# A graph layer on one core: edges and zeros are loaded into the buffers first, and the gathers add onto them

## The chip, the cores and the metric

The kernel runs on one core of a Trainium2 chip. Its time is the device time of one execution in microseconds; before the change the median of three runs is 2434.07 us (2429.45 to 2435.82). The engines of a core work side by side and meet at semaphores: TensorE (PE in the profile, PEld its weight loads), VectorE (DVE), ScalarE (ACT), GpSimd (POOL) and SyncE (SP), which here only issues transfers. Sixteen DMA engines carry the transfers of all of them.

## The reference

A graph with N = 12500 nodes of D = 64 features and E = 212500 edges, sorted by destination, goes through one attention layer:

```
h_trans = x @ Watt.T + Watt_b
e   = sum(h_trans[dst] * tanh(h_trans[src] + edge_attr), axis=-1) / 8
e   = leaky_relu(e, 0.2)
p   = exp(e - segment_max(e, dst)[dst])
alpha   = p / (segment_sum(p, dst)[dst] + 1e-9)
h_neigh = segment_sum(x[src] * alpha, dst)
h   = leaky_relu((x + h_neigh) @ W1.T + W1_b + (x * h_neigh) @ W2.T + W2_b)
out = layernorm(x + h)
```

The term that the change touches is `h_trans[src] + edge_attr`: a gathered row of 64 numbers plus the edge's own row of 64.

## The kernel before, in words

Since the edges are sorted by destination, the kernel walks over blocks of 128 destination nodes, 98 of them. A block takes a window of 19 tiles of 128 edges (MAIN = 17 and TAIL = 2); a tail tile that the block does not need is not gathered. Tiles are worked on in five chunks of four (the last has three), and in three pieces of two chunks each for the coarser steps.

Set-up: x is loaded and copied into hx, TensorE and VectorE compute h_trans, and SP writes a table in HBM whose row n is h_trans of node n (64 numbers) and x of node n (64 numbers), 512 bytes together. A search finds each block's first edge.

The main part is a software pipeline over blocks (`pipeline`, L330). Every engine runs its own `step` or `gather` for each block, four blocks to a turn of a loop, and an engine's order is just the order of its code. In one step it works for several blocks: `b`, the block before it `prev`, the one before that `before`, then `third`, and for `nxt` and `ahead` (b + 1 and b + 2).

- SP (`step`, L455) waits until block b - 2 is scored (`scored`) and its ids are set (`ids_set`). Then it loads the edges of b into one of two buffers `edge` (`load_edges`), the row of destinations of b (`load_row`), and the indices of block b + 2 (`load_indices`).
- GpSimd (`gather`, L543) has four buffers `got`. For each of the 19 tiles it issues one indirect DMA (L560): 128 table rows by the source indices into `got[:, g, 0:128]`. Before chunks 0, 2 and 4 it waits until block n - 4 has been weighted (`weighted`), since that frees the buffer.
- VectorE adds the gathered h_trans onto the edges, chunk by chunk (`add`, L1084), ScalarE takes tanh (`tanh`, L662), and VectorE multiplies by the expanded h_trans[dst] from PSUM and sums (`dot`, L1095). For prev it computes maxima by scans, ScalarE takes the exponential, and VectorE weights the x half of the gathered rows (`weight_rows`, L1143), splits them into three bf16 parts, and TensorE sums them by a one-hot matrix.
- The second half of the gathered row, `got[:, :, 64:128]`, is x[src]; its last column, 128, holds ones.

After the last block the rows are normalised and stored.

Of the kernel before, what the change touches and what calls it, by code (L numbers as in the profile page):

```python
# [22 lines left out]
ALU = mybir.AluOpType  # L23
ACT = mybir.ActivationFunctionType
# [5 lines left out]
P = 128  # L30
MAIN = 17
# [3 lines left out]
BUFS = 4  # L35
# [15 lines left out]
def at_block(turn, k):  # L51

    return Block(turn * BUFS + k, k % BUFS, k % 2, turn + k // BUFS, turn * 2 + k // 2, isinstance(turn, int))


def gnn_layer(nc, x, src, dst, edge_attr, w1, b1, w2, b2, watt, batt, out):
# [31 lines left out]
    with ExitStack() as ctx:  # L88
        def sb(name, shape, dt=F32):
            return ctx.enter_context(nc.sbuf_tensor(name, shape, dt))  # L90
# [4 lines left out]
        def sem(name):  # L95
            return ctx.enter_context(nc.semaphore(name))
# [60 lines left out]

        src_i = [sb(f"src_i{k}", [P, TILES], I32) for k in range(BUFS)]
        dst_i = [sb(f"dst_i{k}", [P, TILES], I32) for k in range(BUFS)]
        edge = [sb(f"edge{k}", [P, TILES, D]) for k in range(2)]  # L160
        got = [sb(f"got{k}", [P, TILES, 2 * D + 1]) for k in range(BUFS)]

# [108 lines left out]
        h3_ready = sem("h3_ready")  # L271

        index_in = [sem(f"index_in{k}") for k in range(BUFS)]
        edge_in = [sem(f"edge_in{k}") for k in range(2)]
        gathered = [[sem(f"gathered{k}_{c}") for c in range(NC)] for k in range(BUFS)]
        row_in = [sem(f"row_in{k}") for k in range(2)]
        hot_built = by_chunk("hot_built")
# [115 lines left out]
        def _(sp):  # L393
# [33 lines left out]
            def first_edge(b):  # L427
                return sp.value_load(start_i[0:1, b.n:b.n + 1] if b.known else start_i[0:1, bass.ds(b.n, 1)],
                                     min_val=0, max_val=E - WINDOW)
# [6 lines left out]
                                 vector[bass.ds(o + MAIN * P, TAIL * P)].rearrange("(g p) -> p g", p=P),  # L436
                                 allow_slow_non_contiguous=True).then_inc(index_in[b.four], 16)

            def load_edges(b, o):
                sp.dma_start(edge[b.two][:, 0:MAIN, :],  # L440
                             edge_attr[bass.ds(o, MAIN * P), :].rearrange("(p g) d -> p g d", g=MAIN))\
                    .then_inc(edge_in[b.two], 16)
                sp.dma_start(edge[b.two][:, MAIN:TILES, :],
                             edge_attr[bass.ds(o + MAIN * P, TAIL * P), :].rearrange("(g p) d -> p g d", p=P))\
                    .then_inc(edge_in[b.two], 16)

            def load_row(b, o):
                ends = dst[bass.ds(o, MAIN * P)].rearrange("(a p g) -> a p g", a=1, g=MAIN)[:, :, 0:MAIN:MAIN - 1]
                sp.dma_start(row_i[b.two][:, 0:2 * P].rearrange("a (p e) -> a p e", e=2), ends,
                             allow_slow_non_contiguous=True).then_inc(row_in[b.two], 16)  # L450
                sp.dma_start(row_i[b.two][:, 2 * P:ROW],
                             dst[bass.ds(o + MAIN * P, TAIL * P)].rearrange("(a n) -> a n", a=1))\
                    .then_inc(row_in[b.two], 16)

            def step(third, before, prev, b, nxt, ahead):  # L455
                if not exists(b):
                    return
                edges_at = first_edge(b)
                indices_at = first_edge(ahead) if exists(ahead) else None
                if follows(b, 2):  # L460

                    sp.wait_ge(scored[NC - 1], b.n - 1)
                    sp.wait_ge(ids_set, b.n - 1)
                load_edges(b, edges_at)
                load_row(b, edges_at)
                if exists(ahead):
                    load_indices(ahead, indices_at)

            def general_tile(t):

# [7 lines left out]
            with sp.If(is_general(sp)):  # L478
# [3 lines left out]
                for k in range(PIECES):  # L482
                    a, z = k * PIECE, (k + 1) * PIECE if k < PIECES - 1 else BLOCKS
                    sp.dma_start(state_piece[k][:, 0:z - a, :],
                                 state[a * P:z * P, :].rearrange("(b p) d -> p b d", p=P)).then_inc(g_back, 16)
            with sp.Else():
                for n in range(2):
                    load_indices(at_block(0, n), first_edge(at_block(0, n)))
                pipeline(sp, step)

            def store(a, z):
# [14 lines left out]
        def _(pool):  # L506
# [9 lines left out]

            for k in range(BUFS):
                pool.memset(got[k][:, MAIN:TILES, 0:2 * D], 0.0).then_inc(consts, 1)

            def place_x(k):  # L520

# [21 lines left out]
            def gather(third, before, prev, b, nxt, ahead):  # L543
                if not exists(b):
                    return
                if follows(b, BUFS):

                    pool.wait_ge(weighted[0], b.n - (BUFS - 1))
                pool.wait_ge(index_in[b.four], (b.fours + 1) * 64)
                n = pool.value_load(count_i[0:1, b.n:b.n + 1] if b.known else count_i[0:1, bass.ds(b.n, 1)],  # L550
                                    min_val=0, max_val=E)
                for c, tiles in enumerate(CHUNKS):
                    if c in (2, 4) and follows(b, BUFS):


                        pool.wait_ge(consts, 11)
                        pool.wait_ge(weighted[c // 2], b.n - (BUFS - 1))  # L557
                    for g in tiles:
                        def rows():
                            pool.indirect_dma_start(got[b.four][:, g, 0:2 * D], None, table,  # L560
                                                    bass.IndirectOffsetOnAxis(ap=src_i[b.four][:, g:g + 1], axis=0))\
                                .then_inc(gathered[b.four][c], 16)
                        if g < MAIN:
                            rows()
                        else:

                            with pool.If(n > g * P):  # L567
                                rows()
                            with pool.Else():
                                pool.inc_swdge_sem([gathered[b.four][c]], [16], mode="add")  # L570
# [42 lines left out]
        def _(act):  # L613
# [44 lines left out]

            def tanh(b, c):
                a, z = cols(c)  # L660
                act.wait_ge(added[c], b.n + 1)
                act.activation(edge[b.two][:, a:z, :], edge[b.two][:, a:z, :], ACT.Tanh).then_inc(tanh_done[c], 1)  # L662

            def set_ids(b):

# [269 lines left out]
        def _(dve):  # L935
# [140 lines left out]
                    dst_rel[:, a:z, :].rearrange("p g (z a) -> p g z a", z=1).to_broadcast([P, z - a, P // 2, 2]),  # L1076
                    ALU.is_equal).then_inc(hot_built[c], 1)

            def add(b, c):
                a, z = cols(c)  # L1080
                if c == 0:
                    dve.wait_ge(edge_in[b.two], (b.twos + 1) * 32)
                dve.wait_ge(gathered[b.four][c], (b.fours + 1) * (16 * (z - a)))
                dve.tensor_tensor(edge[b.two][:, a:z, :], edge[b.two][:, a:z, :], got[b.four][:, a:z, 0:D],  # L1084
                                  ALU.add).then_inc(added[c], 1)

            def dot(b, c):

                a, z = cols(c)
# [112 lines left out]
            def step(third, before, prev, b, nxt, ahead):  # L1202
                if exists(third):
                    residual(third, 0)
                if exists(prev):
                    finish_scores(prev)
                if exists(third):
                    residual(third, 1)
                if exists(b):
                    add(b, 0)  # L1210
                if exists(nxt):
                    place(nxt)
                    build_hot(nxt, 0)
                    build_hot(nxt, 1)
                if exists(prev):
                    scan_row(prev)
                if exists(b):
                    add(b, 1)
                    dot(b, 0)
                if exists(nxt):  # L1220
                    build_hot(nxt, 2)
                    build_hot(nxt, 3)
                    build_hot(nxt, 4)
                if exists(prev):
                    exponents(prev)
                if exists(b):
                    add(b, 2)
                    dot(b, 1)
                if exists(prev):
                    for p in range(NP):  # L1230
                        weight_rows(prev, p)
                if exists(b):
                    add(b, 3)
                if exists(prev):
                    for p in range(NP):
                        rest(prev, 0, p)
                if exists(b):
                    dot(b, 2)
                    add(b, 4)
# [108 lines left out]
```

## Time and profile before

| | |
|---|---|
| median of three runs | 2434.07 us |
| the profiled execution | 2435.8 us |
| its span | 2434.1 us |
| GpSimd busy | 1824.6 us, 75% |
| VectorE busy | 1799.4 us, 74% |
| TensorE busy | 1051.8 us, 43% |
| ScalarE busy | 875.6 us, 36% |
| gathers (L560) | 1716, 1045 ns each |
| additions (L1084) | 490, 407 ns each |

The profile gives for each engine how long it was busy, then the chain of waits: from the last instruction back, at each step to what released it. That chain tells which engine's work sets the end. For a group of instructions the profile gives the number, the busy time, the mean of one, and the idle time of the engine just before them with what ended it. "issue" means that nothing in the profile explains the idle time: the engine was being handed its next instruction, for example.

### The profile page before, as it was taken

The page shows a single profiled execution, that of the slowest core. Times are in us where ns is not written, and L with a number is a line of the kernel's source. Part 1 is how long each engine was busy: PE and PEld are TensorE (multiplying, and loading weights), DVE is VectorE, ACT ScalarE, POOL GpSimd, SP SyncE. Part 2 cuts the span into 40 slices and gives each one's busy share as a digit, 9 for nine tenths or more (in the row PEclk, how much of TensorE's full clock was granted, in tenths as well). Part 3 has the DMA queues.
Part 4 walks back from the last instruction along what each step waited for, and adds up shares of the span by engine and source line. Part 5 has one row for each costly group of instructions (what it writes and reads, how often), then busy time and mean ns, then how long its engine had stood idle before and what let it go on. Part 6 is the DMA issues. An engine that isn't in the chain of part 4 may idle for free.

```text
span 2434.1 us, 41241 instructions
## 1 busy us (share of the span) xinstructions
PE 1051.8 (43%) x10542; PEld 905.3 (37%) x10542; DVE 1799.4 (74%) x8215; ACT 875.6 (36%) x2120; POOL 1824.6 (75%) x1741
## 2 busy tenths in 40 slices
PE   3334444444434444454444454444344444444441
PEld 3334333334433333343333343343343333433331
DVE  5577778678777778687687787787777776877866
ACT  4343333334243333333344243343333333343431
POOL 2777777777777777777777777777777777777773
PEclk8565556655565565556565566566555655666555
DMA  7323323232322323233232332323323232323322
GB/s 193 88 74 78 80 71 81 69 82 70 81 78 71 82 70 82 70 82 80 72 81 70 82 80 70 81 69 81 81 70 81 69 81 70 79 72 79 81 60 55
DMA packets 243239, 191.45 MB, mean 79 GB/s; under 512 B 190278, under 2 KB 202876, under 8 KB 243100
## 3 DMA queue, kind: packets, MB, share of 16 engines
q0 software_dynamic: 55072, 113.24, 17.4%
q1 hardware_dynamic: 188028, 76.98, 13.6%
q14 instruction: 129, 1.06, 0.2%
q8 instruction: 10, 0.16, 0.0%
HBM read 180.47 MB, written 9.60 MB: 78 GB/s over the span
## 4 chain that ended last, share of the span: by engine, by line
POOL 68%; issue 22%; POOLq 7%; SPq 1%; DMA 1%; DVE 1%; PE 0%; ACT 0%; DVEq 0%; ACTq 0%
POOL got L560 67%; POOLq L570 4%; POOLq L550 2%; SPq L422 1%; DMA triple<-in_dst 1%; POOL hx L374 0%; POOLq L567 0%; PE ps_acc L869 0%; POOLq L88 0%; POOL hx L376 0%; POOL hx L524 0%; POOLq L557 0%; DMA got<-table,src_i 0%; POOLq L337 0%; DMA dst_i<-in_dst 0%
## 5 line engine op out<-in xcount | busy, mean ns | idle before, releaser
L560 POOL DMA_INDIRECT got<-table,src_i x1716 | 1794.0, 1045 | 550.3 <-issue 550.3
L662 ACT ACTIVATE edge<-edge 128x256 f32<-128x256 f32 (+1 forms) x490 | 198.2, 404 | 1072.8 <-DVE edge L1084 1063.7
L1084 DVE TENSOR_TENSOR edge<-edge,got 128x256 f32<-128x256 f32 (+1 forms) x490 | 199.3, 407 | 297.2 <-DMA got<-table,src_i 293.8
L876 PE MATMUL ps_misc<-ident,sum_prod 128*128 128x128 f32 x98 | 46.5, 474 | 727.5 <-DVE sum_prod L1172 727.5
L657 ACT ACTIVATE hotT<-ps_hot 128x1024 bf16<-128x1024 bf16 (+1 forms) x294 | 236.6, 841 | 343.6 <-PE ps_hot L817 343.6
L831 PEld LDWEIGHTS ps_hd<-h,hotT 128*128 128x128 bf16 x5586 | 340.4, 134 | 19.5 <-issue 4.9
L831 PE MATMUL ps_hd<-h,hotT 128*128 (+1 forms) x5586 | 338.1, 242 | 4.5 <-DVE raw L1095 4.5
L1095 DVE CUSTOM_DVE_ANT_0 edge<-edge,ps_hd 128x64 f32<-128x64 f32 x1862 | 298.7, 211 | 1.4 <-PE ps_hd L831 0.4
L876 PEld LDWEIGHTS ps_misc<-ident,sum_prod 128*128 128x128 f32 x98 | 17.9, 182 | 747.0 <-DVE sum_prod L1172 747.0
L869 PE MATMUL ps_acc<-triple,hot 128*128 128x195 bf16 x1862 | 295.3, 347 | 0.3 <-DVE z L1178 0.3
L694 ACT ACTIVATE triple<-rows 128x520 bf16<-128x520 f32 (+1 forms) x588 | 284.5, 550 | 14.9 <-DVE rows L1152 11.8
L869 PEld LDWEIGHTS ps_acc<-triple,hot 128*128 128x128 bf16 x1862 | 244.2, 138 | 18.2 <-DVE z L1178 0.5
L817 PE MATMUL ps_hot<-ident,hot 128*128 128x128 bf16 x1862 | 195.1, 275 | 75.8 <-ACT hotT L657 50.9
L1143 DVE TENSOR_TENSOR rows<-got,weight 128x520 f32<-128x520 f32 (+1 forms) x294 | 155.2, 582 | 91.1 <-ACT weight L682 90.7
L817 PEld LDWEIGHTS ps_hot<-ident,hot 128*128 128x128 bf16 x1862 | 170.6, 130 | 96.5 <-issue 69.2
L1073 DVE TENSOR_TENSOR hot<-iota_h,dst_rel 128x512 bf16<-128x512 bf16 (+1 forms) x490 | 174.2, 401 | 3.4
L843 PE MATMUL ps_row<-ident,part_max 128*1 128x128 f32 x196 | 57.4, 396 | 244.1 <-DVE part_max L1109 143.3
L1152 DVE TENSOR_TENSOR rows<-rows,triple 128x520 f32<-128x520 f32 (+1 forms) x294 | 154.6, 579 | 7.7 <-ACT triple L694 7.4
L1155 DVE TENSOR_TENSOR triple<-rows,triple 128x520 bf16<-128x520 f32 (+1 forms) x294 | 154.8, 581 | 0.0
L1095 DVE DVE_READ_ACCUMULATOR2_ANT raw<- 128x1 f32 x1862 | 145.3, 78 | 0.2 <-issue 0.2
L857 PE MATMUL ps_misc<-ident,row_max 1*128 1x1 f32 x196 | 36.1, 251 | 239.5 <-issue 234.8
L857 PEld LDWEIGHTS ps_misc<-ident,row_max 1*128 1x128 f32 x196 | 30.6, 203 | 252.7 <-issue 252.7
(122 smaller groups left out, 1418.6 us busy)
## 6 DMA issues: line engine op xcount, KB each, us to landing
edge<-in_edge_attr SPq DMA_DIRECT2D x98, 544.0 KB
got<-table,src_i POOLq DMA_INDIRECT x1716, 2.5
edge<-in_edge_attr SPq DMA_DIRECT2D x98, 64.0 KB
table<-hx SPq DMA_DIRECT2D x12, 512.0 KB
row_i<-in_dst SPq DMA_DIRECT2D x196, 1.0 KB
got<-in_x SPq DMA_DIRECT2D x3, 768.0 KB, 14.4
src_i<-in_src SPq DMA_DIRECT2D x98, 8.5 KB
src_i<-in_src SPq DMA_DIRECT2D x98, 1.0 KB
```

What stands on the lines that cost most here:

```text
L560: pool.indirect_dma_start(got[b.four][:, g, 0:2 * D], None, table, bass.IndirectOffsetOnAxis(ap=src_i[b.four][:, g:g + 1], axis=0))\
L657: act.activation(hotT[b.two][:, a:z, :], ps, ACT.Copy).then_inc(hot_sb[p], 1)
L662: act.activation(edge[b.two][:, a:z, :], edge[b.two][:, a:z, :], ACT.Tanh).then_inc(tanh_done[c], 1)
L694: act.activation(parts[:, a:z, k, :], rows[:, a:z, :], ACT.Copy).then_inc(part_set[k][p], 1)
L817: last = pe.transpose(ps_hot[(b.two + p) % 2][:, k * P:(k + 1) * P], hot[b.four][:, g, :], ident16[:, :])
L831: last = pe.matmul(expanded(g), hotT[b.two][:, g, :], rhs, start=(part == 0), stop=(part == 2))
L869: last = pe.matmul(a_sum, hot[b.four][:, g, :], triple[:, g, 0:SUMS], start=(g == 0), stop=(g == TILES - 1))
L1073: dve.tensor_tensor(hot[b.four][:, a:z, :].rearrange("p g (n a) -> p g n a", a=2), iota_h[:, :].rearrange("p (z n a) -> p z n a", z=1, a=2 ...
L1084: dve.tensor_tensor(edge[b.two][:, a:z, :], edge[b.two][:, a:z, :], got[b.four][:, a:z, 0:D], ALU.add).then_inc(added[c], 1)
L1095: last = dve.tensor_tensor_reduce(out=edge[b.two][:, g, :], in0=edge[b.two][:, g, :], in1=expanded(g), scale=1.0, scalar=0.0, op0=ALU.mult ...
L1143: dve.tensor_tensor(rows[:, a:z, :], got[b.four][:, a:z, D:2 * D + 1], weight[:, a:z].rearrange("p (g d) -> p g d", d=1).to_broadcast([P, ...
L1155: dve.tensor_tensor(parts[:, a:z, 2, :], rows[:, a:z, :], parts[:, a:z, 1, :], ALU.subtract)\
```

## The change

Edges are no longer loaded into buffers of their own. SP loads them straight into the first 64 columns of the `got` buffer of the block two ahead, and a third transfer copies a row of zeros into its columns 64 to 127 (`lay_edges`, which takes the place of `load_edges`). The gathers now have `compute_op=ALU.add`: they add the table's row onto what lies there. So `got[:, g, 0:64]` becomes h_trans[src] + edge_attr, and `got[:, g, 64:128]` becomes 0 + x[src]. VectorE's `add` is gone; ScalarE's tanh waits for the gathers and reads `got`, writing `edge`, which has to be free (block b - 2 scored). GpSimd waits for the three transfers (`laid`) in place of the freed buffer, and SP now waits for the freed buffer, that is for all pieces of `weighted` of block b - 2, before it loads for block b + 2.

```
-            def load_edges(b, o):
-                sp.dma_start(edge[b.two][:, 0:MAIN, :],
+            def lay_edges(b, o):
+
+                sp.dma_start(got[b.four][:, 0:MAIN, 0:D],
                              edge_attr[bass.ds(o, MAIN * P), :].rearrange("(p g) d -> p g d", g=MAIN))\
-                    .then_inc(edge_in[b.two], 16)
-                sp.dma_start(edge[b.two][:, MAIN:TILES, :],
+                    .then_inc(laid[b.four], 16)
+                sp.dma_start(got[b.four][:, MAIN:TILES, 0:D],
                              edge_attr[bass.ds(o + MAIN * P, TAIL * P), :].rearrange("(g p) d -> p g d", p=P))\
-                    .then_inc(edge_in[b.two], 16)
+                    .then_inc(laid[b.four], 16)
+                sp.dma_start(got[b.four][:, :, D:2 * D],
+                             zeros[:, :].rearrange("p (g d) -> p g d", g=1).to_broadcast([P, TILES, D]))\
+                    .then_inc(laid[b.four], 16)
...
-                    sp.wait_ge(scored[NC - 1], b.n - 1)
+                    sp.wait_ge(zeros_set, 1)
+                    for p in range(NP):
+                        sp.wait_ge(weighted[p], b.n - 1)
                     sp.wait_ge(ids_set, b.n - 1)
-                load_edges(b, edges_at)
-                load_row(b, edges_at)
+                row_at = first_edge(b)
+                ahead_at = first_edge(ahead) if exists(ahead) else None
+                load_row(b, row_at)
                 if exists(ahead):
-                    load_indices(ahead, indices_at)
+                    load_indices(ahead, ahead_at)
+                    lay_edges(ahead, ahead_at)
...
+                sp.wait_ge(x_set, PIECES)
+                sp.wait_ge(zeros_set, 1)
                 for n in range(2):
                     load_indices(at_block(0, n), first_edge(at_block(0, n)))
+                    lay_edges(at_block(0, n), first_edge(at_block(0, n)))
...
-                if follows(b, BUFS):
-
-                    pool.wait_ge(weighted[0], b.n - (BUFS - 1))
+                pool.wait_ge(laid[b.four], (b.fours + 1) * 48)
...
                             pool.indirect_dma_start(got[b.four][:, g, 0:2 * D], None, table,
-                                                    bass.IndirectOffsetOnAxis(ap=src_i[b.four][:, g:g + 1], axis=0))\
-                                .then_inc(gathered[b.four][c], 16)
+                                                    bass.IndirectOffsetOnAxis(ap=src_i[b.four][:, g:g + 1], axis=0),
+                                                    compute_op=ALU.add).then_inc(gathered[b.four][c], 16)
...
-                act.wait_ge(added[c], b.n + 1)
-                act.activation(edge[b.two][:, a:z, :], edge[b.two][:, a:z, :], ACT.Tanh).then_inc(tanh_done[c], 1)
+                act.wait_ge(gathered[b.four][c], (b.fours + 1) * (16 * (z - a)))
+                if follows(b, 2):
+
+                    act.wait_ge(scored[c], b.n - 1)
+                act.activation(edge[b.two][:, a:z, :], got[b.four][:, a:z, 0:D], ACT.Tanh).then_inc(tanh_done[c], 1)
```

On SP, this stood in one step of the pipeline before: the wait, the edges of b, its row, and the first indices of b + 2.

```order
L440 ISA [waits ids_set,scored_4]
L440 DMA edge<-in_edge_attr 128x1088
L443 ISA
L443 DMA edge<-in_edge_attr 128x2x64
L449 REGISTER_ALU
L449 DMA row_i<-in_dst 1x256x1
L451 REGISTER_ALU
L451 DMA row_i<-in_dst 1x256
L433 REGISTER_ALU
L433 DMA src_i<-in_src 128x17
L435 ISA
L435 DMA src_i<-in_src 128x2x1
```

Now the step begins with the wait and the row (the line numbers have moved):

```order
L430 TENSOR_LOAD start_i [waits weighted_2,weighted_1,ids_set,weighted_0,zeros_set]
L430 ISA x2
L430 TENSOR_LOAD start_i
L430 ISA x2
L455 REGISTER_ALU
L455 DMA row_i<-in_dst 1x256x1
```

and it ends with the indices of b + 2 and the three loads of b + 2:

```order
L435 DMA src_i<-in_src 128x17
L437 ISA
L437 DMA src_i<-in_src 128x2x1
L435 DMA dst_i<-in_dst 128x17
L437 DMA dst_i<-in_dst 128x2x1
L443 ISA
L443 DMA got<-in_edge_attr 128x17x64
L446 ISA
L446 DMA got<-in_edge_attr 128x2x64
L449 DMA got<-zeros 128x19x64
```

The wait has moved from the scores of b - 2 to its weighting, and the edges from the front of the step to its end, for a block two later; their form has changed from rows of 1088 numbers to 17 runs of 64.

On VectorE, an early step before: the scores of prev, the first addition of b, the one-hots of nxt, the scans, the second addition, the first score of b (`L1095`).

```order
L1103 SCALAR_TENSOR_TENSOR score<-raw 128x19
L1106 SCALAR_TENSOR_TENSOR run_max<-gap,score 128x17
L1109 SCALAR_TENSOR_TENSOR part_max<-gap,run_max 128x17
L1084 TENSOR_TENSOR edge<-edge,got 128x256
L1062 TENSOR_SCALAR dst_rel<-dst_i,base 128x38
L1065 TENSOR_SCALAR base<-base 128x1
L1073 TENSOR_TENSOR hot<-iota_h,dst_rel 128x512 x2
L1115 SCALAR_TENSOR_TENSOR row_max<-row_gap,ps_row 1x512
L1117 SCALAR_TENSOR_TENSOR row_max<-row_gap,row_max 1x512
L1084 TENSOR_TENSOR edge<-edge,got 128x256
L1095 ISA edge,raw<-edge,ps_hd 128x64
```

The same place now:

```order
L1103 SCALAR_TENSOR_TENSOR score<-raw 128x19
L1106 SCALAR_TENSOR_TENSOR run_max<-gap,score 128x17
L1109 SCALAR_TENSOR_TENSOR part_max<-gap,run_max 128x17
L1070 TENSOR_SCALAR dst_rel<-dst_i,base 128x38
L1073 TENSOR_SCALAR base<-base 128x1
L1081 TENSOR_TENSOR hot<-iota_h,dst_rel 128x512 x2
L1115 SCALAR_TENSOR_TENSOR row_max<-row_gap,ps_row 1x512
L1117 SCALAR_TENSOR_TENSOR row_max<-row_gap,row_max 1x512
L1095 ISA edge,raw<-edge,ps_hd 128x64
```

Only the additions are gone; nothing else on VectorE changes its place. On GpSimd the order of the gathers is the same, with the other waits.

## Rows read from the trace of the kernel before

**Rows 1.** The page, busy time: us, share of the span, instructions.

```profile
PE 1051.8 (43%) x10542; PEld 905.3 (37%) x10542; DVE 1799.4 (74%) x8215; ACT 875.6 (36%) x2120; POOL 1824.6 (75%) x1741
```

**Rows 2.** The page, the chain that ended last, by engine and by line.

```profile
POOL 68%; issue 22%; POOLq 7%; SPq 1%; DMA 1%; DVE 1%; PE 0%; ACT 0%; DVEq 0%; ACTq 0%
POOL got L560 67%; POOLq L570 4%; POOLq L550 2%; SPq L422 1%; DMA triple<-in_dst 1%; POOL hx L374 0%; POOLq L567 0%; PE ps_acc L869 0%; POOLq L88 0%; POOL hx L376 0%; POOL hx L524 0%; POOLq L557 0%; DMA got<-table,src_i 0%; POOLq L337 0%; DMA dst_i<-in_dst 0%
```

**Rows 3.** Groups of GpSimd: count | busy us, mean ns | idle before.

```profile
L560 POOL DMA_INDIRECT got<-table,src_i x1716 | 1794.0, 1045 | 550.3 <-issue 550.3
...
L529 POOL DMA_INDIRECT triple<-in_dst,row_idx x1 | 1.3, 1287 | 16.2 <-issue 16.2
```

**Rows 4.** Line 560: ns min/median/max, first and last start; who waited; landing.

```profile
L560 POOL DMA_INDIRECT got<-table,src_i x1716: 940/944/2311, 57.4 to 2372.8; - x191
...
  DVE edge L1084: 293.8, 152
...
DMA to landing us min/median/max: 2.4/2.5/4.5
```

**Rows 5.** GpSimd in order of time: start us, us, instruction, idle before.

```profile
57.45 1.48 POOL L560 DMA_INDIRECT got<-table,src_i  x1 [27.70 <-issue]
...
1207.80 0.94 POOL L560 DMA_INDIRECT got<-table,src_i  x1 [0.30 <-issue]
1209.05 1.15 POOL L560 DMA_INDIRECT got<-table,src_i  x1 [0.30 <-issue]
1210.50 0.94 POOL L560 DMA_INDIRECT got<-table,src_i  x1 [0.30 <-issue]
```

**Rows 6.** The page, VectorE's additions.

```profile
L1084 DVE TENSOR_TENSOR edge<-edge,got 128x256 f32<-128x256 f32 (+1 forms) x490 | 199.3, 407 | 297.2 <-DMA got<-table,src_i 293.8
```

**Rows 7.** Count loads up to 1200 us, then from 1200; scores up to 1207.

```profile
L550 POOLq TENSOR_LOAD <-count_i x49: 283/290/302, 56.1 to 1180.1; - x49
...
L550 POOLq TENSOR_LOAD <-count_i x5: 285/288/296, 1203.1 to 1296.7; - x5
...
L1103 DVE SCALAR_TENSOR_TENSOR score<-raw x48: 166/169/181, 84.8 to 1206.0; 128x19 f32<-128x19 f32 x48
```

**Rows 8.** VectorE in order of time, parts of one step.

```profile
1208.14 0.43 DVE L1084 TENSOR_TENSOR edge<-edge,got 128x256 f32<-128x256 f32 x1
...
1208.95 0.76 DVE L1073 TENSOR_TENSOR hot<-iota_h,dst_rel 128x512 bf16<-128x512 bf16 x2
1209.63 1.20 DVE L1115 TENSOR_TENSOR_SCAN row_max<-row_gap,ps_row 1x512 f32<-1x512 f32 x1
...
1217.09 1.58 DVE L1143 TENSOR_TENSOR rows<-got,weight 128x520 f32<-128x520 f32 x3 [1.58 <-ACT weight L682]
```

**Rows 9.** SP's transfers of one step, the first and the last of eight.

```profile
1200.66 0.34 SPq L440 DMA_DIRECT2D edge<-in_edge_attr  x1
...
1204.63 0.38 SPq L435 DMA_DIRECT2D dst_i<-in_dst  x1
```

**Rows 10.** Stretches of 256-byte pieces: ..., PEclk, DMA share, GB/s last.

```profile
10.00:15.00 5.00, 0.00 (x0) 0.00 (x0) 0.00 (x0) 0.00 (x0) 0.00 (x0) 1.00 0.97 167
...
2416.00:2420.00 4.00, 0.00 (x0) 0.00 (x0) 3.09 (x1) 0.00 (x0) 3.92 (x2) 0.50 0.96 218
```

**Rows 11.** Stretches about one load of edges, the same columns.

```profile
1200.00:1202.00 2.00, 0.83 (x16) 0.67 (x13) 1.16 (x9) 0.00 (x0) 1.39 (x2) 0.50 0.32 70
1202.00:1204.00 2.00, 0.00 (x0) 0.00 (x0) 0.00 (x0) 0.00 (x0) 1.44 (x2) 0.50 0.92 319
1204.00:1206.00 2.00, 0.00 (x0) 0.00 (x0) 0.11 (x1) 0.00 (x0) 1.64 (x2) 0.50 0.65 99
...
1208.00:1224.00 16.00, 7.04 (x75) 6.07 (x72) 13.70 (x64) 8.34 (x21) 12.50 (x12) 0.71 0.20 49
```

**Rows 12.** The main part as one stretch, the same columns.

```profile
80.00:2370.00 2290.00, 1010.73 (x10214) 869.48 (x10214) 1718.95 (x8012) 828.67 (x2029) 1773.14 (x1697) 0.59 0.30 76
```

**Rows 13.** The page, DMA queues: GpSimd's is q0, SP's is q1.

```profile
q0 software_dynamic: 55072, 113.24, 17.4%
q1 hardware_dynamic: 188028, 76.98, 13.6%
```

**Rows 14.** SP in the set-up: three loads of x, block 0's first index load.

```profile
5.90 15.14 SPq L396 DMA_DIRECT2D got<-in_x  x3
...
52.04 0.37 SPq L433 DMA_DIRECT2D src_i<-in_src  x1
```

More of the change, by code:

```diff
@@ L159, in gnn_layer @@
         dst_i = [sb(f"dst_i{k}", [P, TILES], I32) for k in range(BUFS)]
+        zeros = sb("zeros", [P, D])
         edge = [sb(f"edge{k}", [P, TILES, D]) for k in range(2)]
@@ L273, in gnn_layer @@
         index_in = [sem(f"index_in{k}") for k in range(BUFS)]
-        edge_in = [sem(f"edge_in{k}") for k in range(2)]
+        zeros_set = sem("zeros_set")
+        laid = [sem(f"laid{k}") for k in range(BUFS)]
         gathered = [[sem(f"gathered{k}_{c}") for c in range(NC)] for k in range(BUFS)]
@@ L457, in step @@
                     return
-                edges_at = first_edge(b)
-                indices_at = first_edge(ahead) if exists(ahead) else None
                 if follows(b, 2):
-                    sp.wait_ge(scored[NC - 1], b.n - 1)
+                    sp.wait_ge(zeros_set, 1)
+                    for p in range(NP):
+                        sp.wait_ge(weighted[p], b.n - 1)
                     sp.wait_ge(ids_set, b.n - 1)
-                load_edges(b, edges_at)
-                load_row(b, edges_at)
+                row_at = first_edge(b)
+                ahead_at = first_edge(ahead) if exists(ahead) else None
+                load_row(b, row_at)
                 if exists(ahead):
-                    load_indices(ahead, indices_at)
+                    load_indices(ahead, ahead_at)
+                    lay_edges(ahead, ahead_at)
             def general_tile(t):
@@ L518, in _ @@
                 pool.memset(got[k][:, MAIN:TILES, 0:2 * D], 0.0).then_inc(consts, 1)
+            pool.memset(zeros[:, :], 0.0).then_inc(zeros_set, 1)
             def place_x(k):
@@ L552, in gather @@
                 for c, tiles in enumerate(CHUNKS):
-                    if c in (2, 4) and follows(b, BUFS):
-                        pool.wait_ge(consts, 11)
-                        pool.wait_ge(weighted[c // 2], b.n - (BUFS - 1))
                     for g in tiles:
@@ L1077, in build_hot @@
                     ALU.is_equal).then_inc(hot_built[c], 1)
[L1079 to L1085, printed above, removed]
             def dot(b, c):
@@ L1208, in step @@
                     residual(third, 1)
-                if exists(b):
-                    add(b, 0)
                 if exists(nxt):
@@ L1217, in step @@
                 if exists(b):
-                    add(b, 1)
                     dot(b, 0)
@@ L1226, in step @@
                 if exists(b):
-                    add(b, 2)
                     dot(b, 1)
@@ L1231, in step @@
                         weight_rows(prev, p)
-                if exists(b):
-                    add(b, 3)
                 if exists(prev):
@@ L1238, in step @@
                     dot(b, 2)
-                    add(b, 4)
                 if exists(before):
```

## The prediction

> **What bounds the kernel now.** I read the busy shares and the chain of waits first, then the largest group of the engine that the chain names, then its single instructions, and last the transfers. GpSimd and VectorE are busy for almost the same share, 75% and 74% [rows 1], so the shares do not decide. The chain does: 67% of it is the gather at L560, and 22% is "issue" [rows 2]. There are 1716 gathers, 1045 ns each on average, with 550.3 us of idle time before them [rows 3]. Less the 27.7 us before the first one [rows 5] that is 522.6/1715 = 305 ns a gap. The first gather starts at 57.4 us and the last at 2372.8 [rows 4], and 1716 x 1.045 + 522.6 = 2316 us fills that whole stretch: GpSimd never waits for a buffer there. It issues gathers back to back, 0.94 us and 0.30 us of gap [rows 5]. Around it lie 57 us of set-up and some 60 us of last block and normalisation. VectorE waits for gathers 152 times, 293.8 us together [rows 4]; it is the follower. So the price of this change is what it does to one gather on GpSimd, times 1716, and what it puts ahead of the first gather.
>
> **VectorE's additions.** 490 go, 199.3 us [rows 6]. VectorE follows, so this is worth nothing in the stretch; in the last block it takes off about a microsecond. ScalarE's tanh then waits for the gather itself, one hop less, also beside the gathers. I count 0.
>
> **What GpSimd waits for.** Three waits for free buffers per block become one wait for three loads. Every gap that I see in the stretch is 0.30 us with or without such a wait before it [rows 5], so 0 for their removal. The new wait must be met in time. SP now issues the loads of block n+4 after all three pieces of block n are weighted. Blocks from 0: GpSimd reads the count of block 48 at 1180.1 us, of 49 at 1203.1 and of 53 at 1296.7 [rows 7], so of block 51 at about 1250. VectorE finishes the scores of block 47 at 1206.0 (the 48th) [rows 7] and its weighting at 1217.09 + 1.58 = 1218.7 [rows 8]. SP then issues the row and index loads, which take it about 4 us (the first of its transfers at 1200.66, the last at 1204.63) [rows 9], and then the three loads. With 10 us for these they have landed by 1233, 17 us before they are wanted. A longer gather only widens that. Behind SP's wait are queued the row of block b, wanted by ScalarE at the end of its step, and the indices two blocks ahead; they go some 15 us later than now and still have a block to spare. 0.
>
> **The added transfers.** Edges went as 4352-byte rows (128 x 1088); now they go as 17 pieces of 256 bytes to a partition, with 2 x 64 beside them, and zeros add 19 more. That is (19 + 19) x 128 = 4864 pieces a block, 304 on each of 16 DMA engines. Two places show 256-byte pieces alone. While x is loaded the engines are 97% busy at 167 GB/s: 16 x 0.97 x 256 / 167 = 23.8 ns a piece. While the output is stored they are 96% busy at 218 GB/s: 18.0 ns [rows 10]. So a block's loads hold each DMA engine for 5.5 to 7.2 us. What they replace is the burst at 1200 to 1206: (0.32 + 0.92 + 0.65) x 2 us less the 0.20 of the stretch behind it, 2.6 us [rows 11]. The share over the stretch is 0.30 [rows 12], or 7.1 us of a block of 23.6 us (2316/98). The new load would be 7.1 - 2.6 + 5.5 to 7.2 = 10 to 11.7 us, and if the adding gathers hold the engines twice as long, another 17.4% of the span [rows 13] = 4.1 us: 16 of 23.6. Hidden. SP is free too: 3072 such pieces hold it about 5.05 us (15.14/3) when its queue is full [rows 14], so 4864 take at most 8 us of SP's 23.6.
> Ahead of the first gather nothing hides them. SP starts block 0's index loads at 52.04 us and the first gather starts at 57.45, behind them [rows 5, 14]. Behind those four loads come now the three of block 0: 5.5 to 7.2 us of transfer, and perhaps 2 us more for issue and landing (a gather needs 2.5 to land [rows 4]), part of it beside the indices' own landing. I take 7 us, within 4 to 10.
>
> **The adding gather.** No row shows one. From below: the DMA engines do the addition and GpSimd writes as many instructions for them as now, +0 ns; below nothing is possible only through what runs beside (see the rivals). From above: it has to name twice as many transfers, since the destination is read too, and all of its 944 ns is such naming: +944 ns, 1716 x 0.944 = 1620 us. The nearest row is the other indirect DMA of this kernel, L529: 99 rows of 6800 bytes, 1287 ns [rows 3] where 128 rows of 512 bytes take 944 [rows 4]. It is a gather whose transfers are put together differently from those at L560, and the only one. I take it as the size of what a different form costs: +343 ns, 1716 x 0.343 = 589 us. It is a guess between ends far apart and the largest uncertainty here; +343 sits in the lower half of 0 to 944, which suits a cost of which part must be fixed.
>
> **Sum.** The profiled execution took 2435.8 us in all, 1.7 us above its span and the median of the runs. 2435.8 - 0 + 7 + 589 = 3032, less 1.7: **3030 us**. A block would take 23.6 + 17.5 x 0.343 = 29.6 us, still GpSimd's own time.
>
> **Rivals.**
> *The gather costs what it did.* Then only the 7 us remain: 2434 + 7 = 2441 us. For it: the same 128 rows, the same indices, and an addition done elsewhere. Against it: something has to name the read of the destination. It falls on both sides of 0.3% (7.3 us), which is about what a measurement of this kernel can tell from no change.
> *The gather's naming doubles.* 2434 + 7 + 1620 = 4061 us. For it: with no wait in the stretch, the 944 ns look like work that goes by rows (940 at least, 944 in the median [rows 4]). Against it: a part must be fixed for an instruction.
> The Trainium skill, page "Collectives: The Full Stack", section on the fold count, says that an adding transfer needs two source reads, and that two read descriptors are issued for each chunk where a copy has one. By that rule the time tends to this rival; no row here shows an adding transfer.
> *Faster.* One mechanism: the gathers are longer than their floor because VectorE works beside them. The mean is 1045 ns and the floor 944, 101 x 1716 = 173 us. If VectorE's traffic does that and the additions carry their part of it, 199.3 of 1799.4 us, then 19 us go; less 7, 2422 us. If they carried all of it, 2434 + 7 - 173 = 2268 us. It decides from 7 us on, 4 ns a gather. Against it: the gather at 1207.80 takes 0.94 us with the addition at 1208.14 inside it, and the one at 1209.05 takes 1.15 us with no addition in it but one-hots and a scan [rows 5, 8].
> The Trainium skill, page "SBUF — State Buffer", section "Who interferes with whom", has a two-input addition take only the shared read path, while building descriptors needs the write path. By that rule the trace agrees, and nothing would come back.
> *The DMA engines become the bound.* The adding gathers would have to hold them for more than 23.6 - (11.7 - 4.1) = 16 us a block, where the plain ones hold 4.1: four times as long. At five times, 20.5 + 7.6 = 28 us a block, 98 x 4.5 = 440 us more: 2880 us. For it: each 512-byte row would be fetched, added and written in turn. Against it: 0.30 share now [rows 12].
>
> **How the numbers follow.** Forecast (a gather longer by 50 to 700 ns, own range 2525 to 3640) 0.42; doubled 0.15; unchanged 0.26, half of it within 0.3% and half slower; faster 0.10; the DMA engines as bound 0.07. Slower by over 0.3%: 0.42 + 0.15 + 0.13 + 0.07 = 0.77; within 0.13; faster 0.10. The range goes from 2425, which keeps the unchanged case and a little of the faster one, to 4060, the doubled case; outside are the larger gains and a gather that more than doubles.
>
> **What the changed profile would show.** Right: the gather's floor about 1.29 us at the same 0.30 gap, the chain on it for over two thirds, VectorE's busy time down by 199 us and its waits for gathers up, the first gather about 7 us later, the DMA share at about 0.5 to 0.6 of a shorter block. Wrong: a floor of 0.94 (unchanged), of 1.9 (doubled), a mean nearer the floor (faster), or a DMA share near 1 with gathers that land late and GpSimd held at its wait for the loads.

## The result and the profile after

The changed kernel takes 3353.38 us (median of four runs, 3351.42 to 3357.83), the kernel before 2434.95 us beside it: ratio 1.379, 95% interval 1.3771 to 1.3808. The profiled execution took 3357.83 us, its span 3356.1.

The page of the changed kernel, the busy time and the chain of waits, which answer to [rows 1, 2]:

```profile
PE 1008.5 (30%) x10542; PEld 874.0 (26%) x10542; DVE 1652.1 (49%) x7725; ACT 851.6 (25%) x2120; POOL 2741.4 (82%) x1742
...
POOL 76%; issue 17%; POOLq 4%; PE 1%; DMA 1%; SPq 0%; DVE 0%; ACT 0%; DVEq 0%; ACTq 0%
```

GpSimd carries more of the chain than before (76% for 68%), and VectorE has fallen from 74% to 49% of the span. The gathers (L565 now), in the view of groups and then of the line, which answer to [rows 3, 4] (ns min/median/max, then the first and last start):

```profile
L565 POOL DMA_INDIRECT got<-table,src_i x1716 | 2710.6, 1580 | 558.1 <-issue 558.1
```
```profile
L565 POOL DMA_INDIRECT got<-table,src_i x1716: 1531/1540/2510, 65.3 to 3296.8; - x191
...
  ACT edge L670: 2373.4, 435
...
DMA to landing us min/median/max: 3.1/3.3/6.3
```

The same 1716 gathers take 1580 ns each in place of 1045, and the median 1540 in place of 944. The gaps are the same: 558.1 us less the 35.5 before the first is 522.6 us, as before. Where the 922 us of span went is a sum of three terms, from the first and last start of a gather here and in [rows 4]: the first gather starts 65.3 - 57.4 = 7.9 us later; from the first to the last start it is 3231.5 us in place of 2315.4, 916 us more (1716 x 0.535 = 918); and behind the last start it is 59.3 us in place of 61.3, 2 us less.

GpSimd in order of time, at the start and in the middle (answers to [rows 5]):

```profile
65.32 1.60 POOL L565 DMA_INDIRECT got<-table,src_i  x1 [35.50 <-issue]
...
1501.85 1.54 POOL L565 DMA_INDIRECT got<-table,src_i  x1 [0.30 <-issue]
1503.69 1.54 POOL L565 DMA_INDIRECT got<-table,src_i  x1 [0.30 <-issue]
1505.54 1.96 POOL L565 DMA_INDIRECT got<-table,src_i  x1 [0.30 <-issue]
```

The DMA queues, then the main part as one stretch (the last two columns are DMA share and GB/s), which answer to [rows 13, 12]:

```profile
q0 software_dynamic: 247264, 113.24, 28.0%
q1 hardware_dynamic: 628636, 138.00, 22.3%
```
```profile
80.00:3280.00 3200.00, 970.33 (x10241) 840.57 (x10241) 1571.38 (x7524) 806.15 (x2030) 2682.24 (x1699) 0.58 0.50 73
```

GpSimd's queue moves the same 113.24 MB in 247264 packets in place of 55072: 1716 x 144 against 1716 x 32, with 160 others in both, so 112 packets more for each gather of 128 rows. They hold the engines 0.280 x 3356 = 940 us in place of 0.174 x 2434 = 424 us, 2.2 times as long. Still the share of all transfers over the main part is 0.50, so the engines have half their time free. SP's loads of one block, and how long edges and zeros take to land in the median:

```profile
1511.67 0.60 SPq L443 DMA_DIRECT2D got<-in_edge_attr  x1
1512.45 1.81 SPq L446 DMA_DIRECT2D got<-in_edge_attr  x1
1514.31 0.65 SPq L449 DMA_DIRECT2D got<-zeros  x1
```
```profile
got<-zeros SPq DMA_DIRECT2D x98, 608.0 KB, 6.0
got<-in_edge_attr SPq DMA_DIRECT2D x98, 544.0 KB, 4.9
```

### The profile page after: what moved, and what is told of

Read it like the earlier page. It is cut to its first block, busy times and chain, and to the rows that moved or that the text cites. A ratio compares the mean times of both kernels' runs of the same rounds, so it can differ in the third digit from the quotient of the medians.

```text
span 3356.1 us, 41105 instructions
## 1 busy us (share of the span) xinstructions
PE 1008.5 (30%) x10542; PEld 874.0 (26%) x10542; DVE 1652.1 (49%) x7725; ACT 851.6 (25%) x2120; POOL 2741.4 (82%) x1742
## 3 DMA queue, kind: packets, MB, share of 16 engines
q0 software_dynamic: 247264, 113.24, 28.0%
## 4 chain that ended last, share of the span: by engine, by line
POOL 76%; issue 17%; POOLq 4%; PE 1%; DMA 1%; SPq 0%; DVE 0%; ACT 0%; DVEq 0%; ACTq 0%
POOL got L565 75%; POOLq L575 2%; POOLq L560 1%; DMA triple<-in_dst 0%; POOL hx L376 0%; POOLq L572 0%; PE ps_row L789 0%; PE ps_acc L877 0%; PE ps_hd L789 0%; SPq L424 0%; PE ps_hd L778 0%; DMA got<-zeros 0%; POOLq L88 0%; POOL hx L378 0%; DMA got<-table,src_i 0%
## 5 line engine op out<-in xcount | busy, mean ns | idle before, releaser
L565 POOL DMA_INDIRECT got<-table,src_i x1716 | 2710.6, 1580 | 558.1 <-issue 558.1
L670 ACT ACTIVATE edge<-got 128x256 f32<-128x256 f32 (+1 forms) x490 | 199.3, 407 | 2373.9 <-DMA got<-table,src_i 2373.4
L1095 DVE CUSTOM_DVE_ANT_0 edge<-edge,ps_hd 128x64 f32<-128x64 f32 x1862 | 299.0, 213 | 749.5 <-issue 741.8
L839 PEld LDWEIGHTS ps_hd<-h,hotT 128*128 128x128 bf16 x5586 | 328.8, 132 | 14.4
L839 PE MATMUL ps_hd<-h,hotT 128*128 (+1 forms) x5586 | 324.8, 238 | 0.0
L877 PE MATMUL ps_acc<-triple,hot 128*128 128x195 bf16 x1862 | 282.6, 337 | 0.3 <-DVE z L1178 0.3
L889 PE MATMUL ps_acc<-w12T,sum_prodT 128*128 128x64 f32 x196 | 67.3, 447 | 634.6 <-ACT sum_prodT L706 634.6
L877 PEld LDWEIGHTS ps_acc<-triple,hot 128*128 128x128 bf16 x1862 | 234.2, 133 | 16.8 <-DVE z L1178 0.5
L889 PEld LDWEIGHTS ps_acc<-w12T,sum_prodT 128*128 128x128 f32 x196 | 49.0, 311 | 663.3 <-ACT sum_prodT L706 663.3
L1143 DVE TENSOR_TENSOR rows<-got,weight 128x520 f32<-128x520 f32 (+1 forms) x294 | 155.3, 583 | 68.4 <-ACT weight L690 68.4
L1095 DVE DVE_READ_ACCUMULATOR2_ANT raw<- 128x1 f32 x1862 | 149.3, 80 | 1.3 <-issue 0.7
L1117 DVE TENSOR_TENSOR_SCAN row_max<-row_gap,row_max 1x512 f32<-1x512 f32 x98 | 118.7, 1211 | 3.4
L1115 DVE TENSOR_TENSOR_SCAN row_max<-row_gap,ps_row 1x512 f32<-1x512 f32 x98 | 117.7, 1201 | 0.3 <-PE ps_row L853 0.2
```

The costliest lines, as they stand in the source:

```text
L670: act.activation(edge[b.two][:, a:z, :], got[b.four][:, a:z, 0:D], ACT.Tanh).then_inc(tanh_done[c], 1)
L839: last = pe.matmul(expanded(g), hotT[b.two][:, g, :], rhs, start=(part == 0), stop=(part == 2))
L877: last = pe.matmul(a_sum, hot[b.four][:, g, :], triple[:, g, 0:SUMS], start=(g == 0), stop=(g == TILES - 1))
L1095: last = dve.tensor_tensor_reduce(out=edge[b.two][:, g, :], in0=edge[b.two][:, g, :], in1=expanded(g), scale=1.0, scalar=0.0, op0=ALU.mult ...
L1143: dve.tensor_tensor(rows[:, a:z, :], got[b.four][:, a:z, D:2 * D + 1], weight[:, a:z].rearrange("p (g d) -> p g d", d=1).to_broadcast([P, ...
```

## The experiments

Each comparison has its own runs of the kernel before. They fell into two kinds: in one of them that kernel took 2435.08 us, as above, and in three, each on another chip, 3582.33, 3604.71 and 3615.52 us. So every result below names the kernel before beside it. A time from one kind is set against a time from the other only where GpSimd's gathers fill the run. The median durations of single gathers are read from the traces, and there both kinds agree (944 or 945 ns plain, 1540 or 1541 adding).

**Only the addition undone.** The changed kernel with plain gathers, run twice (e1_laid_plain, e8_laid_plain_again). It leaves the edges out of the scores.

```
-    bass.IndirectOffsetOnAxis(ap=src_i[b.four][:, g:g + 1], axis=0),
-    compute_op=ALU.add).then_inc(gathered[b.four][c], 16)
+    bass.IndirectOffsetOnAxis(ap=src_i[b.four][:, g:g + 1], axis=0)).then_inc(gathered[b.four][c], 16)
```

> The changed kernel with only the addition taken out of the gathers: the three loads per block, SP's wait, GpSimd's wait and the missing VectorE additions all stay. It leaves out the edges in the scores, since the plain gather overwrites them. Theory (the whole cost is the form of the gather on GpSimd): a gather takes its 0.94 us again, mean at most 1.05 us, the first gather stays at 65.3 us, time 2435 + 8 = 2443 us. Rival (the added loads or the new waits cost something in the loop): gathers with a mean above 1.1 us or gaps above 0.30 us, time above 2480 us. Second rival (VectorE's additions had lengthened the gathers): mean near 1.00 us, time near 2370 us.

Measured the first time: 3546.41 us beside 3582.33, ratio 0.9909 (0.986 to 0.9957). The waits view of this run (us in total, times, the longest):

```profile
ACT hotT L662 <- PE ps_hot L825: 2123.2, 88, 49.5
POOL got L565 <- issue: 1699.1, 1712, 40.2
```

ScalarE waited 2123 us for TensorE, and GpSimd had 1700 us of gaps, with gathers of 945 ns in the median: something else was the bound, so the run says nothing on the sum. The same kernel was run again.

> The same kernel as the first experiment (the changed kernel with plain gathers; it leaves the edges out of the scores), because the kernel before itself took 3582 us on the chip of that comparison in place of 2434, with TensorE idle for 'issue' between single matmuls. Theory (the form of the gather is the whole cost, and that chip had a limit of its own beside GpSimd): where the kernel before takes about 2434 us, this takes 2443 us, a gather 0.94 us at the least and 1.0 us on average (998 ns were seen), gaps 0.30 us. With a mean of 998 in place of 1045 ns it could be 1716 x 0.047 = 81 us less, 2362 us, if the additions had lengthened the gathers. Rival (the loads and the new wait cost something): above 2480 us.

Measured: 2419.71 us beside 2435.08, ratio 0.9938 (0.9916 to 0.9959). The gathers:

```profile
L565 POOL DMA_INDIRECT got<-table,src_i x1716: 940/945/1822, 65.0 to 2359.5; - x191
```
```profile
L565 POOL DMA_INDIRECT got<-table,src_i x1716 | 1772.7, 1033 | 557.9 <-issue 557.6 <-DMA got<-zeros 0.3
```

The whole loss is gone, with all loads, both new waits and the missing additions in place. The new wait for the loads cost GpSimd 0.3 us in 98 blocks. The expected time was 2443 us, so 23 us less than that, and 15 us less than the kernel before: gathers of 1033 in place of 1045 ns, 1716 x 0.012 = 21 us, less the 7.6 us by which the first gather starts later (65.0 us for 57.4). What shortened them this run does not tell, since the additions are gone and the loads have moved as well.

**Only the addition put in.** The kernel before with `compute_op=ALU.add` in its gathers, and the four buffers cleared once ahead; it adds onto what the buffer held.

```
+            for k in range(BUFS):
+                pool.memset(got[k][:, :, 0:2 * D], 0.0).then_inc(cleared, 1)
+            pool.wait_ge(cleared, BUFS)
...
-                                                    bass.IndirectOffsetOnAxis(ap=src_i[b.four][:, g:g + 1], axis=0))\
+                                                    bass.IndirectOffsetOnAxis(ap=src_i[b.four][:, g:g + 1], axis=0), compute_op=ALU.add)\
```

> The kernel before with only the addition put into the gathers (and the four buffers cleared once ahead, some 10 us on GpSimd). It adds onto what the buffer held, so rows pile up; edges still go to their own buffers and VectorE still adds. Theory (the form of the gather is the whole cost): floor of 1.54 us, mean 1.58 to 1.64 us, time 2435 + 10 + 1716 x (0.535 to 0.60) = 3363 to 3475 us. Rival (half of the loss comes from the loads, waits or the 256-byte pieces): mean near 1.3 us, time near 2900 us.

Measured: 3358.97 us (two runs) beside 3582.33, ratio 0.9375 (0.9357 to 0.9393): the kernel before was of the slower kind there. The comparison that counts is with the changed kernel, 3353.38 us, from which it differs by 0.2%; that kernel keeps its time from chip to chip (last experiment). It lies just under the 3363 us that I had expected at the least. The gathers:

```profile
L564 POOL DMA_INDIRECT got<-table,src_i x1716 | 2707.1, 1578 | 524.9 <-issue 517.9 <-DVE rows L1147 7.0
```

With the two together, the form of the gather is the cost, and it alone makes the loss. VectorE's additions are still there and the mean is 1578 ns, where it is 1580 without them and with the new loads: beside adding gathers these two changes together give nothing.

**What the cost of an adding gather goes by.** The same two kernels (buffers cleared ahead) with gathers of 64 and of 16 rows, the other rows left out, and one with adding gathers of 128 rows of 256 bytes, which fetch x in place of the table. This is the edit for 64 adding rows:

```
-                            pool.indirect_dma_start(got[b.four][:, g, 0:2 * D], None, table,
-                                                    bass.IndirectOffsetOnAxis(ap=src_i[b.four][:, g:g + 1], axis=0))\
+                            pool.indirect_dma_start(got[b.four][0:64, g, 0:2 * D], None, table,
+                                                    bass.IndirectOffsetOnAxis(ap=src_i[b.four][0:64, g:g + 1], axis=0), compute_op=ALU.add)\
```

> The kernel before with each gather fetching 64 rows in place of 128 (the other half of each tile is left out), buffers cleared once ahead. It shows which part of the 944 ns goes by rows. If all of it goes by rows: a floor of 472 ns; if it is fixed for the instruction: 944 ns. I expect about 650 ns, which would be 350 ns fixed and 4.6 ns a row; GpSimd would then still be the bound or nearly, with a time of 1900 to 2100 us where VectorE's own 20 us a block allow it.

> The same with the adding gather: 64 rows, buffers cleared once ahead, rows pile up. If the added 596 ns of the floor (1.54 against 0.944 us) go by rows (a second read is named for every row), the difference to the plain gather of 64 rows is 298 ns, floor about 0.95 us. If they are fixed for an adding instruction, the difference is 596 ns, floor about 1.25 us.

> The kernel before with adding gathers that fetch rows of 64 numbers (256 bytes) from x in place of 128 from the table, 128 rows each; buffers cleared once ahead. It leaves out the h half. If the cost goes by instruction and row, the floor stays at 1.54 us and the time at 3359 us; if it goes by bytes (the transfer holds GpSimd up), the floor falls towards 1.25 us.

> The kernel before with gathers of 16 rows (the other 112 of each tile left out), buffers cleared once ahead. The plain gather took 944 ns for 128 rows and 908 for 64. A straight line gives 872 ns + 0.56 a row: 881 ns here. If the line is not straight (work in groups of rows), something else, down to 600 ns.

> The same with adding gathers of 16 rows. They took 1540 ns for 128 rows and 1412 for 64; a straight line gives 1284 ns + 2.0 a row: 1316 ns here, that is 412 ns fixed and 1.4 ns a row more than the plain one. If what the addition costs goes by rows after all, near 900 ns.

The line of the gathers in these five, in this order (ns min/median/max):

```profile
L564 POOL DMA_INDIRECT got<-table,src_i x1716: 902/908/1506, 63.3 to 3472.5; - x191
```
```profile
L564 POOL DMA_INDIRECT got<-table,src_i x1716: 1403/1412/2385, 64.2 to 3128.1; - x191
```
```profile
L564 POOL DMA_INDIRECT got<-in_x,src_i x1716: 1531/1540/2720, 64.2 to 3310.8; - x191
```
```profile
L564 POOL DMA_INDIRECT got<-table,src_i x1716: 842/848/2211, 64.3 to 2225.1; - x191
```
```profile
L564 POOL DMA_INDIRECT got<-table,src_i x1716: 1307/1317/2386, 64.5 to 2946.6; - x191
```

| rows in a gather | plain, ns | adding, ns | difference |
|---|---|---|---|
| 16 | 848 | 1317 | 469 |
| 64 | 908 | 1412 | 504 |
| 128 | 944 | 1540 | 596 |

The adding form costs 469 ns more already at 16 rows and only 127 beyond that at 128: four fifths of what the addition costs are there at 16 rows and look fixed for the instruction. For 64 rows I had set 298 ns (by rows) against 596 (fixed); 504 lies between, nearer to fixed. The straight line gave 1316 for 16 adding rows (1317 measured) but 881 for 16 plain ones (848). My 650 ns for 64 plain rows was far off. Bytes do not matter to the adding gather: half-width rows take the same 1540 ns. Nor is it the number of packets. At 16 rows GpSimd's queue has 55072 of them in both forms (plain first), and the adding gather still takes 469 ns longer:

```profile
q0 software_dynamic: 55072, 14.84, 2.7%
```
```profile
q0 software_dynamic: 55072, 14.84, 5.1%
```

The times were 3587.23, 3191.02, 3373.57, 2287.56 and 3009.51 us; the first two stood beside 3582.33 us for the kernel before, the others beside 2435.08. Each of the five is a single run. Even 16 plain rows bring the kernel only to 2288 us: with a gather of 955 ns on the mean (848 in the median) and a gap of some 300, GpSimd is still the bound.

**A dose.** The changed kernel with the addition in even tiles only (odd tiles lose their edges).

```
-                                                    compute_op=ALU.add).then_inc(gathered[b.four][c], 16)
+                                                    compute_op=ALU.add if g % 2 == 0 else ALU.bypass).then_inc(gathered[b.four][c], 16)
```

> The changed kernel with the addition only in the gathers of even tiles, some 890 of the 1716 (odd tiles lose their edges). If each adding gather costs its own 1580 - 1033 = 547 ns on GpSimd and nothing else, 2420 + 890 x 0.547 = 2907 us. If a change between the two forms costs something, or the DMA side of an adding gather holds up the next one, more than that: over 2950 us.

Measured: 2929.79 us (one run) beside 3604.71. Line, queue, and three gathers in order of time:

```profile
L565 POOL DMA_INDIRECT got<-table,src_i x1716: 978/1532/2388, 65.5 to 2868.9; - x191
```
```profile
q0 software_dynamic: 153968, 113.24, 23.7%
```
```profile
1501.88 1.54 POOL L565 DMA_INDIRECT got<-table,src_i  x1 [0.30 <-issue]
1503.73 0.98 POOL L565 DMA_INDIRECT got<-table,src_i  x1 [0.30 <-issue]
1505.02 1.72 POOL L565 DMA_INDIRECT got<-table,src_i  x1 [0.31 <-issue]
```

(153968 - 55072)/112 = 883 gathers add. Against the 2419.7 us of the changed kernel with plain gathers, each costs (2929.8 - 2419.7)/883 = 578 ns, 31 above the expected 547. The shortest gather takes 978 ns in place of 940, so a plain one behind an adding one seems to pay some 38 ns, and 833 x 0.038 = 32 us would be the whole of that excess (27 us). Otherwise the cost is simply the number of adding gathers.

**The zeros left out.** The changed kernel without the third load (x piles up in the second half, which is cleared once ahead; GpSimd waits for two transfers in place of three).

```
-                sp.dma_start(got[b.four][:, :, D:2 * D],
-                             zeros[:, :].rearrange("p (g d) -> p g d", g=1).to_broadcast([P, TILES, D]))\
-                    .then_inc(laid[b.four], 16)
```

> The changed kernel without the load of zeros: 98 of the 294 added loads and half of their pieces are left out (rows of x pile up in the second half of the buffers, which are cleared once ahead). If the loads lie beside the gathers, only the first gather moves, 2 to 3 us earlier, and the time is 3350 us with a gather of 1540 ns at the least and 1580 on average. If the loads lengthen the gathers, the mean falls towards 1560 ns or below and the time to 3320 us or less.

Measured: 3353.61 us (one run) beside 3604.71, first gather at 62.6 us, mean 1579 ns. The loads of zeros lie beside the gathers; only those of block 0 hold one up, the first, by 2.7 us, and the time is within the changed kernel's own range.

**The additions left out.** The kernel before with no addition anywhere: tanh waits for edges and gathers. The five calls of `add` are gone too:

```
-                act.wait_ge(added[c], b.n + 1)
+                if c == 0:
+                    act.wait_ge(edge_in[b.two], (b.twos + 1) * 32)
+                act.wait_ge(gathered[b.four][c], (b.fours + 1) * (16 * (z - a)))
```

> The kernel before with VectorE's additions left out and nothing put in their place (edges are still loaded into their own buffers, and the scores lack the gathered rows); tanh waits for the edges and the gathers. With plain gathers and the new loads the kernel took 2419.7 us beside 2435.1, a gather 1033 ns on average in place of 1045. If that gain comes from the additions (they lengthen the gathers beside them) and the new loads cost only the later first gather (7.6 us), this takes 2419.7 - 7.6 = 2412 us with a mean near 1033 ns. If it comes from the loads' new place (SP's loads two blocks ahead, no burst of edge rows beside the gathers), this takes 2434 us with a mean of 1045 ns.

Measured: 3605.18 us beside 3604.71, ratio 1.0004 (0.9994 to 1.0013). It fell on a chip where GpSimd is not the bound of plain gathers, so it does not tell whether the 21 us of the earlier run came from the additions or from the moved loads. Where TensorE's time went in this run (idle time before L833, the matmuls that expand h_trans[dst] to the edges; weight loads and matmuls together, then the matmuls alone):

```profile
  issue: 2592.5, 1564
```
```profile
PE ps_hd L833 <- issue: 1253.1, 780, 6.5
```

**The changed kernel on another chip.**

> The changed kernel itself, unaltered, beside the kernel before, wherever it lands. Theory: its time is 1716 gathers of 1.58 us and gaps of 0.30 us on GpSimd, which no chip has changed so far, so 3353 us everywhere. The kernel before takes 2435 us on one kind of chip (ratio 1.377) and 3582 to 3605 us on the other, where TensorE waits for 'issue' between its matmuls under plain gathers; there the ratio is 3353/3593 = 0.933 and TensorE shows no such waits in the changed kernel. Rival: the changed kernel falls into the same waits there and takes 3600 us or more.

Measured: 3359.75 us beside 3615.52, ratio 0.9293 (0.9277 to 0.9308). Its gathers:

```profile
L565 POOL DMA_INDIRECT got<-table,src_i x1716 | 2712.6, 1581 | 558.0 <-issue 558.0
```

The changed kernel takes the same as on the first chip within 0.2%, and there it is the faster of the two.

## Why the prediction was right

The forecast was 3030 us, slower, with its own range from 2525 to 3640; 3353 lies in it. The mechanism was right. That the number fell into the range owes much to the range's width (50 to 700 ns a gather), since the one large term was a guess. Point by point:

- *GpSimd's gathers are the bound, and the price is that of one gather times 1716.* Shown: plain gathers in the changed kernel take the loss away, adding gathers in the kernel before make all of it.
- *The adding gather, +343 ns.* The mechanism was right and this term was too small: +535 ns on the mean, 918 us in place of 589. The error is 329 us, nearly all of 3353 - 3030. The row that I sized it by, L529, says nothing on additions. My reason for the lower half, that part of a gather must be fixed, did not lead there: 848 ns of a plain gather's 944 are left at 16 rows, and the addition brings 469 of its own beside them. What GpSimd does in these 469 ns no run shows.
- *The naming doubles* (rival). Not so: 1.63 times the floor, and four fifths of the addition's cost do not go by rows. On the DMA engines the time is 2.2 times as long, and at 16 rows, with as many packets in both forms, 0.051 x 3008 = 153 us in place of 0.027 x 2286 = 62 us, 2.5 times. The rule of the Trainium skill (page "Collectives: The Full Stack", section on the fold count) that an addition reads two sources goes in that direction; no trace here shows the second read by itself, and the naming on GpSimd did not double.
- *VectorE's additions, 0.* Right beside adding gathers (1578 ns with them, 1580 without). Beside plain gathers 21 us came back with additions and old loads gone, near the 19 us that the "faster" rival set for the additions' share. That is no proof of it. Counted over the single instructions of the kernel before, 277 gathers have no VectorE work beside them, and all of these take 953 ns or less: so the time above the floor does come beside VectorE's work, as the rival said. But of the 69 gathers that have an addition beside them and otherwise at most the ids (L1062, L1065) or the scores' products (L1095), 63 take 947 ns or less; the other six, 953 to 1112 ns, are ones that began 100 to 300 ns after their addition. The order seems to decide: of the 104 gathers with only the weighting (L1143) beside them, the 39 that began before it take 953 ns or less, and the 65 that began while it ran take 1257 ns on the mean. So where little else runs beside them the additions lengthen few gathers, and whether they brought the 21 us stays open, as no run varied this alone. The rule of the Trainium skill (page "SBUF — State Buffer", section "Who interferes with whom"), by which nothing would come back, fits the gathers that began first, and not the 6 and the 65 that began beside a running VectorE instruction with two inputs.
- *The waits, 0, and the loads hidden.* Right: 0.3 us of waiting for the loads in 98 blocks with plain gathers, a DMA share of 0.50 where I had 0.5 to 0.6. Two signs that I named came out otherwise. The engine that waits for the gathers is now ScalarE (2373.4 us), not VectorE, since tanh takes them first. And VectorE's busy time fell by 1799.4 - 1652.1 = 147 us, not by the additions' 199: their records overlap those of their neighbours (the one at 1208.14 lasts to 1208.57 [rows 8], and the next record begins at 1208.48), so that all other VectorE work of the kernel before covers 1655 us by itself.
- *Ahead of the first gather, 7 us.* Measured 7.9.
- *The DMA engines as the bound.* No: half of their time is free, and half-width rows change nothing.

## What to carry to other kernels

An addition within a gather is not free for the engine that issues it: GpSimd pays about half a microsecond for each instruction, at 16 rows (469 ns) nearly as at 128 (596 ns). Ask first which engine's instructions set the pace. Here the work was taken from the engine that waits and given to the one that is waited for. And since most of a gather is there at 16 rows already (848 of 944 ns plain, 1317 of 1540 adding), smaller gathers help hardly; fewer gathers should help more, which no run here tried.

## What the runs showed of the hardware that was not expected

- A plain indirect gather of 16 rows takes 848 ns, of 128 rows 944 ns; the gap to the next is 0.30 us in each form. With no VectorE work beside it the gather of 128 rows takes 953 ns at most (277 gathers of the kernel before).
- An adding gather moves its data in 112 more packets for 128 rows, in none more for 16.
- The kernel before took 2435 us in two comparisons and 3582, 3605 and 3616 us in three others on other chips, its runs within 0.4% of each other in each. In the traces from there of kernels with plain gathers, the median gather is as long as on the first chip, but TensorE stands still between single matmuls of the expansion, for "issue", that is, for nothing that the profile shows. The kernel before has two such waits at L831, 4.9 us together, on the first chip. The kernel without additions has 1564 on such a chip (above, weight loads and matmuls counted together). The first line below is of the kernel before, the other two show two of the 1564:

```profile
  issue: 4.9, 2
```
```profile
1536.58 0.21 PE L833 MATMUL ps_hd<-h,hotT 128*128 x1 [2.58 <-issue]
1539.39 0.21 PE L833 MATMUL ps_hd<-h,hotT 128*128 x1 [2.60 <-issue]
```

  With adding gathers in all tiles or in every other one these waits are all but absent on those chips (10.8 us in the kernel before with only the addition put in, 3.2 us with every other tile, none in the changed kernel), and the kernels take what GpSimd's sum gives. So the sign of this change differs from one comparison to the other: 1.379 on one chip, 0.929 on another. What holds TensorE up there, whether it is the chip itself, and why it goes away where gathers take longer, stays open; there is no trace of the kernel before itself on such a chip.
